# An indexed load that moves nothing, issued ahead of the first gather of w1 and ahead of the last stores

## The reference, cut to what matters

```python
rates = relu(inputs) * DT
c = initial_state[:, None, :] + cumsum(rates, axis=1)
fl = floor(c)
spikes = (fl - prev) / DT                      # prev: fl one step earlier
logits = x_flat @ router_w.T
top_v, top_i = top_k(softmax(logits), 2)       # gates: top_v over their sum
h = gelu(einsum('ech,ehf->ecf', expert_in, w1))
y = einsum('ecf,efh->ech', h, w2)
out = out + tok * (gate * keep)                # for both choices
return x + out
```

## Time and profile before

| | us |
|---|---|
| three timed runs | 67.09, 68.56, 68.94 |
| their median | 68.56 |
| profiled execution, its own time | 67.18 |
| its span in the trace | 65.5 |
| PE busy | 53.0 |
| DVE busy | 36.2 |
| ACT busy | 25.9 |
| POOL busy | 18.2 |

### The profile page before, as it was taken

How to read it: one execution, slowest core, us unless ns; L and a number is a source line. 1 busy time by engine, 2 the same in 40 slices (tenths; PEclk the granted TensorE clock), 3 DMA queues, 4 the chain that set the end, 5 groups by cost and what they waited for, 6 DMA issues and landing times.

```text
span 65.5 us, 1291 instructions
## 1 busy us (share of the span) xinstructions
PE 53.0 (81%) x435; PEld 32.7 (50%) x435; DVE 36.2 (55%) x165; ACT 25.9 (39%) x60; POOL 18.2 (28%) x55
## 2 busy tenths in 40 slices
PE   3985999999679971199979999999999999994000
PEld 1312434554345661144539668986597666661000
DVE  0377097877799677988668924867061022026000
ACT  0599425756770039409996300681027002000000
POOL 6799943000002500306668810000000000000740
PEclk9999999999999998555599999999999999999985
DMA  0499999999999999700487860698899991000030
GB/s 0 119 362 320 353 329 355 370 336 344 345 349 348 351 350 343 219 13 0 105 190 228 326 234 35 134 357 283 264 381 384 382 358 35 0 0 0 15 126 10
DMA packets 13545, 14.82 MB, mean 226 GB/s; under 512 B 652, under 2 KB 13046, under 8 KB 13536
## 3 DMA queue, kind: packets, MB, share of 16 engines
q1 hardware_dynamic: 12608, 12.62, 59.4%
q0 software_dynamic: 816, 2.01, 9.9%
q10 hardware_dynamic: 112, 0.07, 0.5%
HBM read 13.08 MB, written 2.36 MB: 236 GB/s over the span
## 4 chain that ended last, share of the span: by engine, by line
PE 63%; ACT 8%; DVE 7%; DMA 7%; issue 5%; POOL 3%; ACTq 2%; POOLq 0%; DVEq 0%
PE bank L662 22%; PE bank L646 12%; PE bank L501 11%; DMA w_got<-in_L_ffn_w_dram,w_index 7%; PE bank L552 6%; POOL out_dram L476 3%; ACT w_got L753 3%; PE bank L507 3%; PE bank L518 2%; PE bank L678 2%; ACT L753 2%; ACTq L749 1%; PE bank L567 1%; PE bank L679 1%; ACT limit L790 1%
## 5 line engine op out<-in xcount | busy, mean ns | idle before, releaser
L662 PE MATMUL bank<-w_sb,spare_sb 128*64 128x256 f32 x128 | 14.7, 382 | 0.0
L662 PEld LDWEIGHTS bank<-w_sb,spare_sb 128*64 128x64 f32 x128 | 8.8, 137 | 4.5
L488 PE MATMUL bank<-ones_b 128*128 128x512 bf16 x23 | 9.4, 555 | 1.1 <-POOL ones_b L380 1.1
L501 PE MATMUL bank<-rate,cum_seq 128*128 128x512 f32 x16 | 8.4, 604 | 0.1
L476 POOL DMA_INDIRECT out_dram<-floors,out_index x2 | 2.0, 1020 | 22.9 <-DVE floors L1092 22.6
L646 PE MATMUL bank<-ev_pair,w_got 128*128 128x128 f32 x64 | 7.8, 278 | 0.4 <-DMA w_got<-in_L_ffn_w_dram,w_index 0.4
L770 ACT ACTIVATE spikes<-bank 128x256 bf16<-128x256 f32 x16 | 6.0, 381 | 5.3 <-PE bank L518 5.2
L646 PEld LDWEIGHTS bank<-ev_pair,w_got 128*128 128x128 f32 x64 | 7.4, 192 | 0.9 <-DMA w_got<-in_L_ffn_w_dram,w_index 0.9
L902 DVE TENSOR_SCALAR floors<-bank 128x512 bf16<-128x512 f32 x8 | 5.5, 691 | 3.5 <-PE bank L507 3.2
L783 ACT ACTIVATE spare_sb<-bank 128x512 f32<-128x512 f32 x8 | 4.8, 597 | 6.7 <-PE bank L646 6.6
L996 DVE TENSOR_SCALAR rate<-bank,pair_gate 128x256 f32<-128x256 f32 x4 | 1.9, 484 | 9.2 <-PE bank L662 9.2
(11 more groups left out here) (176 smaller groups left out, 79.2 us busy)
## 6 DMA issues: line engine op xcount, KB each, us to landing
w_sb<-in_L_ffn_w_dram SPq DMA_DIRECT2D x8, 1024.0 KB, 11.3
x_sb<-in_x_dram SPq DMA_DIRECT2D x8, 256.0 KB, 4.1
out_dram<-x_sb SPq DMA_DIRECT2D x1, 2048.0 KB, 13.7
cond<-in_cond_dram ACTq DMA_DIRECT2D x2, 32.0 KB, 2.3
w_got<-in_L_ffn_w_dram,w_index POOLq DMA_INDIRECT x4, 5.8
cond<-in_cond_dram SPq DMA_DIRECT2D x1, 32.0 KB, 1.9
x_rows<-in_x_dram,out_index POOLq DMA_INDIRECT x2, 3.7
out_dram<-floors,out_index POOLq DMA_INDIRECT x2, 2.8
```

Source lines behind the costliest of these rows:

```text
L488: nc.tensor.matmul(bank[2][:, 0:4 * P], ones_b[:, :], ones_b[:, :].unsqueeze(1).to_broadcast([P, 4, P]), start=True, stop=True)
L501: nc.tensor.matmul(CUM[g % 4][:, 0:GW], cum_seq[:, :], rate[:, g % RING, :, :].rearrange("p j c -> p (j c)"), start=True, stop=False)
L662: mm = nc.tensor.matmul(Y[d % 2][at, :], hT[:, d % 2, f, at], w2_sb[:, 2 * d + side, f, :], start=(f == 0), stop=(f == FC - 1))
```

## The change

POOL gets a function `load_nothing()`: an indexed load of rows of `x` by `far_index`, so that all its 128 indices are out of bounds. Its destination `sink` is a part of `rate` that is not read at that time. It is issued twice: once behind `off_has`, with no wait of its own, ahead of `gather(0)`; and once ahead of the two stores, when the fourth `project` is done (`y_ready` at `D`). A new semaphore `sunk` counts its landings: the second issue waits for the first one's landing, and POOL's end for the second one's.

```diff
+        sink = rate[:, 2, 0, :]
...
+        sunk = sem("sunk")
...
             g.tensor_tensor(off_has[:, :, :, :], has[:, :, :].unsqueeze(2).to_broadcast([P, ST, E, JE]),
                             offset[:, :].unsqueeze(1).unsqueeze(3).to_broadcast([P, ST, E, JE]), ALU.mult).then_inc(off_set, 1)
 
+            def load_nothing():
+
+                g.indirect_dma_start(
+                    out=sink, out_offset=None, in_=x_in_rows[:, :],
+                    in_offset=bass.IndirectOffsetOnAxis(ap=far_index[:, 0:1], axis=0),
+                    bounds_check=N - 1, oob_is_err=False, compute_op=ALU.bypass).then_inc(sunk, 16)
+
+            load_nothing()
+
             def gather(d):
...
             pool.wait_ge(copied, 16)
+            pool.wait_ge(sunk, 16)
+            pool.wait_ge(y_ready, D)
+            load_nothing()
             for t in range(ST):
                 pool.wait_ge(out_set, t + 1)
                 g.indirect_dma_start(
                     out=out_rows[:, :], out_offset=bass.IndirectOffsetOnAxis(ap=out_index[:, t:t + 1], axis=0),
...
+            pool.wait_ge(sunk, 32)
             pool.wait_ge(added, 16 * ST)
```

## The result

| | kernel before | changed kernel |
|---|---|---|
| single runs, us | 67.09, 67.55, 68.56, 68.94, 69.10, 69.47 | 69.24, 69.61, 70.52, 71.42, 72.04, 73.64 |
| median | 68.75 | 70.97 |
| profiled execution / its span | 67.18 / 65.5 | 69.24 / 67.5 |

The ratio is 1.033 with a 95% interval of 1.028 to 1.038: slower, where no difference was forecast. Every ratio here is made of the fastest runs of each kernel alone, because single runs of one kernel spread by 2 us and more. 70.97 lies outside the stated range of 66.5 to 69.3.

A forecast was written before the change was run, and what follows sets the result against it. The kernel was taken as bound by PE (81% busy, 63% of the chain); a gain of 0.11 us, the middle of 0 to 0.22 at first gather and store, came off the 68.56 median, giving 68.4, range 66.5 to 69.3.

The forecast's parts named there:

- The start times of the loads: First gather and first store on POOL: start 0.85 to 0.89 behind release, so at most 0.03 and 0.04 us gained.
- rival one: POOL prepares faster right after a load: gather 0.43 and store 0.44 us earlier, 0.87 in all; chance 0.13.
- a first use after a pause: Reason considered for the first gather lasting 1.11 against 0.99 later: warming saves 0.12 there, 0.02 to 0.03 at the store.
- The empty loads hidden: Empty loads end at about 28.8 and 59.7 to 60.0, before gather and store can start, with 0.3 to 0.6 us spare.
- rival two: First empty load delays DVE masks or `ev_info`, or POOL prepares gather or store only after it: 0.2 to 0.9 us; chance 0.15.
- the one at 30.36: DVE mask beside the first gather, 480 ns instead of 250: sign that a POOL load can hold up a mask by 0.23.
- a gap of 0.62: Largest gap between gathers, replacing 0.30 behind the second empty load at its worst end; put at 0.04 us cost.
- The landing: First gather's data, 4.42 us from start to landing, taken as unchanged; the empty load's completions ahead of it counted as 0.
- The chance of 0.06 for slower by over 2%: Probability given to the whole kernel getting slower by more than 2%, beside 0.88 for same and 0.06 for faster.

The follow-up runs named there:

- e5: Kernel before plus one empty load behind POOL's `to_slot`, about 22.2 us, none ahead of the stores; 68.14 beside 69.06, too few runs for a verdict.
- e7: Kernel before plus two empty loads in a row ahead of the first gather, none ahead of the stores; 69.65 beside 69.06, too few runs for a verdict.
- e10: Kernel before plus two one-column memsets on idle POOL at about 10 us, no empty load; 69.00 beside 68.56, ratio 1.014.
- e6: Kernel before plus one empty load directly behind the early load, about 10.5 us, none ahead of the stores; 69.04 beside 69.06, too few runs.
- e11: Kernel before with the early load left out and the first empty load in its place, ahead of the first gather; 68.50, ratio 0.998.
- e12: Changed kernel, both empty loads, with the early load of the kernel before left out; 68.64 beside 68.56, ratio 1.019.
- e4: Changed kernel measured again, unaltered; 68.85 beside 68.34 for the kernel before, ratio 1.009.
- e8: Kernel before plus only the second empty load, ahead of the stores, as a repeat; 68.59 beside 69.06, too few runs for a ratio.
- e9: Kernel before with the second gather also waiting for the third index list, no empty load; 68.13 beside 68.56, ratio 1.004.
- e14: Kernel before plus four one-column memsets (fillers) on POOL behind the early load, no empty load; ran once, 69.57.
- e15: Changed kernel, both empty loads, plus four one-column memsets (fillers) behind the early load; ran once, 69.20.
- e18: Changed kernel with both empty loads and four one-column memsets (fillers), timed; 68.29 beside 68.76 for the kernel before, ratio 0.987.
- e17: Changed kernel measured a third time, unaltered; 69.64 beside 68.76 for the kernel before, ratio 1.020.
- e1: Kernel before plus one semaphore that nothing raises or waits for, no empty load; 67.84 at the median, ratio 0.997.
- e13: Kernel before plus six one-column memsets (fillers) on POOL behind the early load, no empty load; 68.47 beside 68.38, ratio 0.997.

## Why the prediction was wrong

**The start times of the loads: right.** The first gather started 0.85 behind its list (30.51 to 31.36) right behind a load that had ended 0.82 earlier, so rival one falls. The store started 0.83 behind the addition, for 0.89. The gather lasted 1.00 for 1.11. The gains are 0.03 + 0.11 and 0.06 + 0, in all 0.20, where 0.11 was taken between bounds of 0 and 0.22. The reason that the prediction gave for the shorter gather, a first use after a pause, was not the right one (see e5).

**The empty loads hidden: right.** The first started at 29.28, 0.49 behind `off_has` (0.61 was taken), and ended at 30.54, with the list ready at 30.51. In the forecast's terms it ended 1.75 behind `off_has`, at 28.85 on its scale, where 28.8 was taken. The list was ready 1.72 behind `off_has`, for 1.75, so this chain was not held up and rival two falls in both its forms. A mask of 0.44 to 0.50 beside the first gather, as the one at 30.36 that rival two was built on, comes back in nine more traces, and none beside an empty load. e7 shows where rival two begins to be true: a second empty load costs 0.5 to 0.7. One sum of the prediction is off: with a gap of 0.62 the second empty load would cost 0.07 at the worst end (60.04 + 0.62 - 60.59), not 0.04; nothing rests on it.

**The landing: the step that failed.** The sum left the 4.42 us from the first gather's start to its landing as they were, and put the completions ahead of it at 0. It became 4.70, and 4.62 to 4.80 in six of the seven traces with the hole ahead of the second gather, where it is 4.10 to 4.42 in the traces with the hole ahead of neither gather. Against the 4.42 this cost 0.2 to 0.4 and ate the gain of 0.14. The prediction looked for reasons in what a load does (ports, masks, queues) and never at what it is: two more instructions in a stream. e10 shows it with two memsets; e5 and e6 with a load far off; e11 and e12 by taking two instructions out again. The change costs 0.22 and 0.20 us in the stretch by its own first trace and e4's, against the 7.70 of the kernel before. The four-filler version of it gains 0.3 against the same 7.70, but only 0.1 against e8's 7.47. The lowest single runs point the same way: in the five kernels with the hole ahead of the second gather they are 67.27 to 67.83, and 66.90 to 67.14 in all the others with four runs or more but two, e12 (67.90) and e7 (68.04), whose second empty load delays the gather.

**How the hole delays the landing** is argued, not shown. e9 excludes the late second gather as the link. A gather's landing is the last of 16 completions, and the delay is in that last one alone: in e10, whose trace kept all 16, the 15th comes at 4.19 and the 16th at 4.63, in the kernel before at 4.16 and 4.43, in e9 at 4.14 and 4.24. The DMA record has an instruction packet of 8 KB near it. In the six traces with the late landing the packet starts 2.6 to 3.5 us behind the gather, and 3.5 to 4.2 behind it in the seven with the hole behind the second gather. In e7, e14, e15 and e18, where the hole falls ahead of the first gather, it starts before the gather does, and the landing is 4.21 and 4.04 where the chain shows it (e14, e18). The Trainium skill says in "Runtime: NRT & Kernel Launch", "Instruction fetch mechanics", that each engine's sequencer refills its instruction memory in 16 KiB blocks by its own DMA queue, and that crossing a block boundary costs one DMA tail-bump, "mostly hidden". A hole at a fixed place in the program and a packet behind it agree with that, though the packets near the hole are of 8 KB; that one of the sixteen DMA engines carries the packet ahead of the gather's last rows would explain one late completion, but no trace here tells which engine carried what. e17 is against a strict link: it has the hole and the packet at 3.4, and PE starts its first `hidden` 4.20 behind the gather.

**The size: between the profiled executions mostly not the change.** 1.69 of the 2.07 us between them are the late start. Of the seven traces of kernels with no added load (the kernel before, e1, e9, and those with fillers only) five have the late clock; the kernel before itself left one trace, an early one. The lowest of the changed kernel's first six runs (69.24) is the profiled one, with a late start; the profiled execution of the kernel before (67.18) has an early one, and its two lowest runs (67.09, 67.55) are of that length, though no trace shows their start. So the ratio most likely sets late starts against early ones, which is luck and no property of the change. Over three measurements the medians differ by 2.2, 0.5 and 0.9 us. The prediction saw a spread of 1.9 us in three runs and widened its range for it, but took it as noise without a place. Its one trace could not have told it; a second trace with the other start would have.

**What stays open.** Times above 70.2 came in 6 of the changed kernel's 24 runs, and in 1 of 83 of the kernel before. In the other kernels with an empty load they came in 3 of 65 runs (two of e7, one of e18), and in none of 37 of those with no added load. Four of the nine are from the first measurement. Traces with a stall of 1.6 to 2.3 us on ACT or DVE (e13, e17, e7) may be what such runs look like, but e13 has no empty load; what stalls the engine isn't shown, nor why long runs would come more often with the empty loads. So 0.2 to 0.4 us of the change's cost are explained by the hole, and the rest of the 0.5 to 2.2 between medians is not. The chance of 0.06 for slower by over 2% left no room for a rival of this kind.

## What to carry to other kernels

An instruction added to an engine's stream shifts everything behind it, and a gap of 0.4 us at a fixed place in the stream can move from a wait, where it is free, to the critical path; before crediting or blaming what an added instruction does, add as many harmless ones and look. Where single runs of one kernel fall into two groups, take more than one trace, find where the groups part, and compare kernels stretch by stretch behind that place. A wait-to-start time that is nearly the same after a long and a short pause (0.85 to 0.89 here) is not a cold start; a load issued ahead took no more than 0.06 off it.

## What the runs showed of the hardware

- POOL's sequencer stops for 0.39 us between the 68th and 69th instruction that a trace of this program lists for it, whatever they are: seen as 1.16 for 0.77 (e14), and as 1.23 to 1.25 for 0.85 ahead of a second gather in seven traces. Where POOL waits for something longer there, nothing of it shows.
- How long an indexed load occupies POOL goes with the instruction ahead of it: 0.99 to 1.03 behind another load, also after 19 to 23 us without one, and 1.10 to 1.32 behind a computation or a memset, in all twenty traces. Its start lies 0.83 to 0.91 behind the release; a load that ended shortly before takes 0.03 to 0.06 off.
- An indexed load with every index out of bounds is no shorter on POOL (0.99 to 1.32) than one that moves 0.4 MB (0.99 to 1.11), and lands 2.1 to 2.4 us after its start when the queues are idle, 5.8 to 6.6 when they are full.
- An indexed load's landing is the last of 16 completions, and one of them can come 0.4 us behind the 15th (e10).
- TensorE's clock rises to 2.4 GHz at 4.3 to 5.3 us in some executions and at 8.9 to 10.4 in others, after the same eight warm-up matmuls. Both come in one and the same kernel (the changed one); PE's first two matmuls of `cumulate` then take 1.13 or 1.9 to 2.1, and `has` comes 1.1 to 1.4 us later.
- An engine can stand still for 1.6 to 2.3 us with nothing in the trace to release it (ACT in e13 and e17, DVE in e7).
